# A ViT tower on one core: in the delta-rule stages, all projections ahead of the small products

## The chip, the cores and the metric

One core of a Trainium2 chip runs the whole program in one launch. The metric is the device time in microseconds (us), the median of the runs. TensorE (PE in the rows) multiplies, VectorE (DVE), ScalarE (ACT) and GpSimd (POOL) do the rest. Each works through its own list of instructions in order and waits on semaphores.

## The reference

64 images are cut into 36 patches each, embedded to 256 numbers, and get two class tokens ahead, so that there are 64 x 38 = 2432 tokens. Two layers follow. The first is causal attention and a gated mixture of eight experts, and the second, which the change touches, is a delta-rule recurrence and a ternary feed-forward block:

```python
def step(S, inp):
    qt, kt, vt, at, gkt = inp
    Sp = S * jnp.exp(gkt)[..., None]
    u = jnp.einsum('bhk,bhkv->bhv', at, Sp) + vt
    S = Sp + jnp.einsum('bhk,bhv->bhkv', kt, u)
    o = jnp.einsum('bhk,bhkv->bhv', qt, S)
    return (S, o)
...
q = silu(x @ Wq)
k = silu(x @ Wk)
v = silu(x @ Wv)
log_f = jax.nn.log_sigmoid(x @ Wf)
gamma = -jax.nn.sigmoid(x @ Wgamma)
...
a = k * gamma[..., None] * jnp.exp(gk)
out = dplr_delta_rule(q, k, v, a, gk)
```

Here k is brought to length 1 per head, gk is log_f for all 16 numbers of a head, and there are 16 heads and 38 steps.

## The kernel before

The recurrence isn't run step by step. For a pair of images and a head, the 38 steps form a triangular system, whose inverse is built row by row on VectorE (two blocks of 19 rows) and applied with small products on TensorE. The 64 images go in 8 chunks of 8 images (304 tokens). `last_layer` (line 1202) calls `delta_stage` (line 1402) eleven times, k = 0 to 10, and one stage works on four chunks at once, at different depths:

- chunk `nxt` = k: the projections of keys, queries, gamma and the forget gate. `project(n)`, n = 0 to 7, is 6 products of 128x128 by 128x304 each (line 1474), into bank 6 or 7 of the accumulators in turn. ScalarE takes the sigmoid (`sigmoid(n)`, line 1704); for n = 0 to 3 VectorE multiplies bank and sigmoid (`silu_of`, line 1856). A bank is free for the project two later when that is done: `project` 2 to 5 waits for `silu`, 6 and 7 wait for `sig`. ScalarE also copies the chunk's tokens in padded form for the next stage's values (`padded`, lines 1767 and 1769), and `key_norm` (line 1483) sums the squared keys.
- chunk `c` = k-1: `values(p)` (24 products of 128x128 by 128x272, line 1492), `sigmoid_values` (line 1694), `values_of` (line 1867), the logs of the forget gate, `decay(b)` (lines 1504 and 1506, then an exponential at line 1722), `score(p)` (line 1528) and the product of score and decay, `weigh` (line 1902).
- chunk `z` = k-2: `a_rows` (line 1549) turns the system's matrix, `inverse_row(t)` (lines 1837 and 1840) builds the inverse, and `inverse_out` with `inverse_back` (lines 1564, 1738) turn it round.
- chunk `y` = k-3: the small products. `first_half(0)` and `(1)` (line 1581) apply the first block of the inverse; ScalarE takes the result out (`first_back`, line 1746); `remainder` (line 1593) takes it to the second block; VectorE adds the values (`with_values`, line 1912); `second_half` (line 1605) applies the second block; ScalarE puts the solution in place (`solution`, line 1755) over zeros that GpSimd sets (`clear_pairs`, line 2028); `output()` (line 1621) multiplies by the queries, and `high_out` and `low_out` (lines 1777, 1922) store the sum as a high and a low part.

Stages 3 to 7 hold all four chunks. Stage 0 has only `nxt`, and stages 1 and 2 lack the small products. Stage 8 has the small products and no projections, and stages 9 and 10 hold only what is left of the last chunks. Stage 0 also computes the low-rank gate of all tokens (`low_part`, line 1539, and `low_high`, line 1730). Between stages stands a barrier of all engines.

The order within an engine is written out by hand as a list of calls: lines 1625 to 1664 for TensorE, 1781 to 1819 for ScalarE, 1950 to 1990 for VectorE, 2041 to 2063 for GpSimd. TensorE's:

```python
            first_half(0)
            first_half(1)
            project(0)
            low_part(1)
            remainder(0)
            project(1)
            low_part(2)
            remainder(1)
            project(2)
            low_part(3)
            second_half(0)
            project(3)
            low_part(4)
            second_half(1)
            project(4)
            project(5)
            output()
            project(6)
            project(7)
```

Each float32 product is shown in the trace as two weight loads and two products, so that the 64 products of `remainder(0)` are rows of x128.

Of the kernel before, what the change touches and what calls it, by code (L numbers as in the profile page):

```python
# [45 lines left out]
IP = CB // 2  # L46
# [1355 lines left out]
def delta_stage(nc, psum, bank, buffers, c, nxt, z, y):  # L1402
# [44 lines left out]
    with stage(nc, "dproj", "sig", "silu", "k_sq", "k_n2", "k_max", "k_log", "k_inv",  # L1447
# [13 lines left out]
        def _(pe):  # L1461
# [71 lines left out]
            def low_part(i):  # L1533
                if not first:
                    return
                passes = [x for k in range(HALVES) for x in split_products(
                    wgh[:, k, :], wgl[:, k, :], XH[:, k, spans[i]], XL[:, k, spans[i]])]
                for n, (left, right) in enumerate(passes):
                    mm = nc.tensor.matmul(bank[i][0:HD, 0:spans[i].stop - spans[i].start], left, right,
                                          start=(n == 0), stop=(n == len(passes) - 1))  # L1540
                mm.then_inc(g1_ready, 1)
# [84 lines left out]
            for p in range(IP):  # L1626
                values(p)
            low_part(0)
            first_half(0)
            first_half(1)  # L1630
            project(0)
            low_part(1)
            remainder(0)
            project(1)
            low_part(2)
            remainder(1)
            project(2)
            low_part(3)
            second_half(0)
            project(3)  # L1640
            low_part(4)
            second_half(1)
            project(4)
            project(5)
            output()
            project(6)
            project(7)
            key_norm(0)
            key_norm(1)
            decay(0)  # L1650
# [16 lines left out]
        def _(act):  # L1667
# [74 lines left out]
            def first_back(j):  # L1742
                if y is None:
                    return
                act.wait_ge(u1_done, j + 1)
                nc.scalar.activation(RX[:, lanes(j), :], bank[j][:, :].rearrange("p (l d) -> p l d", d=HD),
                                     ACT.Copy).then_inc(u1_back, 1)
# [36 lines left out]
                forget_parts(p)  # L1784
            forget_logs()
            nc.scalar.preload_act_table_set("sigmoid_and_others")
            first_back(0)
            sigmoid_values(0)
            sigmoid_values(1)
            first_back(1)  # L1790
            sigmoid_values(2)
            sigmoid_values(3)
            sigmoid(0)
            sigmoid(1)
            padded(0)
            sigmoid(2)
            padded(1)
            sigmoid(3)
            for i in range(len(spans)):
                low_high(i)  # L1800
            solution(0)
            solution(1)
            sigmoid(4)
            sigmoid(5)
            high_out(0)
            high_out(1)
            sigmoid(6)
            sigmoid(7)
            nc.scalar.preload_act_table_set("natural_log_exp_and_others")
            inverse_norms()  # L1810
            decay(0)
# [10 lines left out]
        def _(dve):  # L1822
# [129 lines left out]
            for t in range(1, 6):  # L1952
                inverse_row(t)
            log_forget()
            inverse_row(6)
            with_values(0)
            silu_of(0)
            inverse_row(7)
            with_values(1)
            silu_of(1)  # L1960
            values_of(0)
            values_of(1)
            inverse_row(8)
            silu_of(2)
            values_of(2)
            values_of(3)
            inverse_row(9)
            silu_of(3)
            gate_parts()
            for t in range(10, 14):  # L1970
                inverse_row(t)
            low_out(0)
# [20 lines left out]
        def _(pool):  # L1993
# [49 lines left out]
                    keys_in_pair(m, e)  # L2043
            steps(0)
            steps(1)
            clear_pairs(0)
            square(0)
            clear_pairs(1)
            square(1)
            if first:  # L2050
                pool.wait_ge(k_sq, HALVES)
                for n, part in enumerate((0, 2)):
# [190 lines left out]
```

## Time and profile before

| | |
|---|---|
| median of 3 runs | 2023.65 us (2023.57 to 2025.52) |
| the profiled execution: its own time | 2023.33 us |
| its span in the trace | 2021.3 us |
| TensorE busy | 1769.4 us (88%) |
| VectorE busy | 1084.5 us (54%) |
| ScalarE busy | 672.3 us (33%) |
| GpSimd busy | 299.6 us (15%) |
| mean granted clock of TensorE | 0.876 |
| delta stages 0 to 10 | about 1305 to 1800 us of the span |

The span is the trace of one execution; 2.0 us lie around it. A granted clock of 1.00 is 2.4 GHz and 0.50 is 1.2 GHz.

### The profile page before, as it was taken

To read this page: it belongs to the slowest core of one execution; us is meant where nothing else is said; L and a number is where in the kernel's file an instruction comes from. 1 tells how busy PE (TensorE), PEld (TensorE's weight loads), DVE (VectorE), ACT (ScalarE), POOL (GpSimd) and SP (SyncE) were. 2 spreads that over 40 slices of the span, in tenths; PEclk is the share of its full clock that TensorE was granted. 3 is DMA by queue.
4 is the path that set the end of the run, shared out by engine and by line. 5 is a ranking of instruction groups with operands and counts; after the bars stand their busy time and mean duration, and the time that the engine had idled before them with its cause. 6 is when DMAs were issued, how large, how long until landed. Compare 5 with 4: busy or idle time off the path is not lost. (4 is left out here: it accounts for less than half of the span.)

```text
span 2021.3 us, 52149 instructions
## 1 busy us (share of the span) xinstructions
PE 1769.4 (88%) x22817; PEld 1573.1 (78%) x22817; DVE 1084.5 (54%) x2346; ACT 672.3 (33%) x1389; POOL 299.6 (15%) x302
## 2 busy tenths in 40 slices
PE   5677786799999999999999999778999889777589
PEld 4466675579888999999999989566788778767468
DVE  3655555584546545545555455545534454442885
ACT  3344444432223222223223232354333333223133
POOL 0322232610000000000000000332222222100540
PEclk9788898899999999999999999788776877655579
DMA  4100000100001000000000000100000000001001
GB/s 142 50 2 1 0 0 2 65 21 22 22 1 43 1 22 21 22 22 22 22 21 22 1 1 1 34 2 2 3 4 3 3 3 4 4 4 47 1 7 44
DMA packets 9943, 36.03 MB, mean 18 GB/s; under 512 B 3056, under 2 KB 5896, under 8 KB 7176
## 3 DMA queue, kind: packets, MB, share of 16 engines
q1 hardware_dynamic: 9736, 32.96, 4.7%
q8 instruction: 167, 2.74, 0.6%
q14 instruction: 40, 0.33, 0.1%
HBM read 30.47 MB, written 2.49 MB: 16 GB/s over the span
## 5 line engine op out<-in xcount | busy, mean ns | idle before, releaser
L1042 ACT ACTIVATE hidden<-bank,moe_b 128x512 f32<-128x512 f32 (+1 forms) x320 | 213.3, 668 | 537.1 <-PE bank L934 526.1
L951 PE MATMUL bank<-moe_w2h,hidden_hi 128*128 128x256 f32 x1216 | 345.7, 284 | 0.0
L951 PE MATMUL bank<-moe_w2l,hidden_hi 128*128 128x256 f32 x1216 | 344.0, 283 | 0.0
L951 PE MATMUL bank<-moe_w2h,hidden_lo 128*128 128x256 f32 x1216 | 344.0, 283 | 0.0
L934 PE MATMUL bank<-x_hi,moe_w1h 128*128 128x512 f32 (+1 forms) x640 | 243.8, 381 | 2.9 <-ACT hidden L1042 2.8
L934 PE MATMUL bank<-x_lo,moe_w1h 128*128 128x512 f32 (+1 forms) x640 | 242.5, 379 | 0.0
L934 PE MATMUL bank<-x_hi,moe_w1l 128*128 128x512 f32 (+1 forms) x640 | 242.0, 378 | 0.0
L951 PEld LDWEIGHTS bank<-moe_w2h,hidden_hi 128*128 128x128 f32 x1216 | 233.1, 192 | 5.9 <-DVE residual L1076 4.3
L951 PEld LDWEIGHTS bank<-moe_w2l,hidden_hi 128*128 128x128 f32 x1216 | 233.2, 192 | 1.2
L951 PEld LDWEIGHTS bank<-moe_w2h,hidden_lo 128*128 128x128 f32 x1216 | 233.2, 192 | 0.0
L1076 DVE SCALAR_TENSOR_TENSOR residual<-bank,gates,residual 128x256 f32<-128x256 f32 x152 | 73.4, 484 | 290.4 <-PE bank L951 290.4
L1064 DVE TENSOR_TENSOR hidden_lo<-hidden,hidden_hi 128x512 fp32r<-128x512 f32 (+1 forms) x320 | 215.2, 672 | 11.0
L1062 DVE CAST hidden_hi<-hidden 128x512 fp32r<-128x512 f32 (+1 forms) x320 | 133.1, 416 | 87.3 <-ACT hidden L1042 79.9
L934 PEld LDWEIGHTS bank<-x_hi,moe_w1h 128*128 128x128 f32 x640 | 120.3, 188 | 25.8 <-ACT hidden L1042 5.0
L934 PEld LDWEIGHTS bank<-x_hi,moe_w1l 128*128 128x128 f32 x640 | 120.1, 188 | 20.4
L934 PEld LDWEIGHTS bank<-x_lo,moe_w1h 128*128 128x128 f32 x640 | 120.3, 188 | 18.7
L1249 POOL MEMSET gate_low<- 80x2432 f32 x1 | 2.1, 2121 | 867.1 <-POOLq L68 867.1
L167 PE MATMUL bank<-ident,normed_tiles 128*128 128x128 f32 x152 | 49.7, 446 | 47.6 <-DVE normed_tiles L136 47.6
L167 PEld LDWEIGHTS bank<-ident,normed_tiles 128*128 128x128 f32 x152 | 22.5, 204 | 74.1 <-DVE normed_tiles L136 74.0
L2008 POOL TENSOR_TENSOR decay_steps<-normed_tiles,from_here 128x304 f32<-128x304 f32 x64 | 50.5, 804 | 139.6 <-PE bank L1506 73.9
L1902 DVE TENSOR_TENSOR qk_and_ak<-bank,decay 128x304 f32<-128x304 f32 x128 | 52.2, 466 | 22.5 <-ACT decay L1722 17.0
L831 POOL TENSOR_TENSOR probs<-probs,row_inv 128x608 f32<-128x608 f32 x32 | 38.7, 1209 | 167.1 <-DVE row_inv L715 166.9
(284 smaller groups left out, 3531.5 us busy)
## 6 DMA issues: line engine op xcount, KB each, us to landing
moe_w<-in_moe_w SPq DMA_DIRECT2D x16, 1024.0 KB, 4.8
patches<-in_patches SPq DMA_DIRECT2D x8, 864.0 KB, 4.5
out<-residual SPq DMA_DIRECT2D x19, 128.0 KB, 1.7
ffn_w<-in_ffn_w SPq DMA_DIRECT2D x2, 1024.0 KB, 6.4
att_w<-in_att_w SPq DMA_DIRECT2D x1, 1536.0 KB, 5.9
delta_w<-in_delta_w SPq DMA_DIRECT2D x1, 1280.0 KB
tok_w<-in_tok_w SPq DMA_DIRECT2D x1, 768.0 KB, 4.1
delta_wvf<-in_delta_wvf SPq DMA_DIRECT2D x1, 272.0 KB
```

Source lines behind the costliest of these rows:

```text
L167: turn = nc.tensor.transpose(bank[t % 4][:, m * P:(m + 1) * P], XN[:, t % 4, m * P:(m + 1) * P], ident[:, :])
L831: nc.gpsimd.tensor_tensor(PR[:, p % 2, :, 0:SEQ], PR[:, p % 2, :, 0:SEQ], spread(RI[:, p % 2, :], 2, SEQ), ALU.mult).then_inc(normed, 1)
L934: mm = nc.tensor.matmul(bank[i % 4][:, 0:n], left, right, start=(j == 0), stop=(j == len(passes) - 1))
L951: mm = nc.tensor.matmul(bank[4 + n % 3][:, 0:D], left, right, start=(i == 0), stop=(i == len(passes) - 1))
L1042: nc.scalar.activation(H[:, i % 4, 0:n], bank[i % 4][:, 0:n], ACT.Relu, bias=b1[:, x, f:f + 1]).then_inc(acted, 1)
L1062: nc.vector.tensor_copy(HH[:, k % 2, f, 0:n], H[:, i % 4, 0:n]).then_inc(h_hi, 1)
L1064: nc.vector.tensor_tensor(HL[:, k % 2, f, 0:n], H[:, i % 4, 0:n], HH[:, k % 2, f, 0:n].bitcast(F32), ALU.subtract).then_inc(h_lo, 1)
L1076: nc.vector.scalar_tensor_tensor(out=RES[:, t, :], in0=bank[4 + n % 3][:, 0:D], scalar=G[:, t, x:x + 1], in1=RES[:, t, :], op0=ALU.mult, o ...
L1249: nc.gpsimd.memset(G1[:].bitcast(F32), 0.0).then_inc(done, 1)
L1902: nc.vector.tensor_tensor(PA[:, c % 2, p, m * HPH:(m + 1) * HPH].rearrange("p (g e) x t -> p e g x t", e=2)[:, e], psum[:, 0:PPH, n * 2 * ...
L2008: nc.gpsimd.tensor_tensor(MS[:, b % 2], spread(LZ[:, 3, b // 2, b % 2 * HPH:(b % 2 + 1) * HPH], 2, SEQ), spread(here[:, :], 1, HPH), ALU.m ...
```

## The change

No instruction is added or taken away. The four lists of calls in `delta_stage` get another order.

- TensorE: all eight projections follow the values (in stage 0 they alternate with `low_part` as before). Then come the small products without anything between them, and then norms, decays and scores as before.
- ScalarE: `sigmoid(0)` to `(3)` alternate with the sigmoids of the values, `sigmoid(4)` to `(7)` follow, and then `padded` and `first_back`.
- VectorE: `silu_of(0)` to `(3)` move ahead among the rows of the inverse, and `with_values` and `values_of` come after row 8.
- GpSimd: both squares of the keys stand ahead of both `clear_pairs`.

```diff
@@ TensorE @@
             low_part(0)
+            project(0)
+            low_part(1)
+            project(1)
+            low_part(2)
+            project(2)
+            low_part(3)
+            project(3)
+            low_part(4)
+            for n in range(4, 8):
+                project(n)
             first_half(0)
             first_half(1)
-            project(0)
-            low_part(1)
             remainder(0)
-            project(1)
-            low_part(2)
             remainder(1)
-            project(2)
-            low_part(3)
             second_half(0)
-            project(3)
-            low_part(4)
             second_half(1)
-            project(4)
-            project(5)
             output()
-            project(6)
-            project(7)
             key_norm(0)
@@ ScalarE @@
-            first_back(0)
             sigmoid_values(0)
+            sigmoid(0)
             sigmoid_values(1)
-            first_back(1)
+            sigmoid(1)
             sigmoid_values(2)
+            sigmoid(2)
             sigmoid_values(3)
-            sigmoid(0)
-            sigmoid(1)
-            padded(0)
-            sigmoid(2)
-            padded(1)
             sigmoid(3)
             for i in range(len(spans)):
                 low_high(i)
+            for n in range(4, 8):
+                sigmoid(n)
+            padded(0)
+            first_back(0)
+            first_back(1)
+            padded(1)
             solution(0)
             solution(1)
-            sigmoid(4)
-            sigmoid(5)
             high_out(0)
             high_out(1)
-            sigmoid(6)
-            sigmoid(7)
@@ VectorE @@
             log_forget()
+            silu_of(0)
             inverse_row(6)
-            with_values(0)
-            silu_of(0)
+            silu_of(1)
+            silu_of(2)
             inverse_row(7)
-            with_values(1)
-            silu_of(1)
-            values_of(0)
-            values_of(1)
-            inverse_row(8)
-            silu_of(2)
-            values_of(2)
-            values_of(3)
-            inverse_row(9)
             silu_of(3)
             gate_parts()
+            inverse_row(8)
+            with_values(0)
+            with_values(1)
+            for p in range(IP):
+                values_of(p)
+            inverse_row(9)
@@ GpSimd @@
+            square(0)
+            square(1)
             clear_pairs(0)
-            square(0)
             clear_pairs(1)
-            square(1)
```

TensorE's instructions in stage 4 (and in stages 3 and 5 to 7 alike), before, from the last value product on. One row of line 1474 is one product of a projection, and x128 of line 1581 is both first halves:

```order
L1492 MATMUL bank<-delta_wvfh,dchunk_lo 128x272
L1581 MATMUL bank<-values,inverse_t 32x16 x128
L1474 MATMUL bank<-x_hi,delta_wh 128x304
L1474 MATMUL bank<-x_lo,delta_wh 128x304
L1474 MATMUL bank<-x_hi,delta_wl 128x304
L1474 MATMUL bank<-x_hi,delta_wh 128x304
L1474 MATMUL bank<-x_lo,delta_wh 128x304
L1474 MATMUL bank<-x_hi,delta_wl 128x304
L1593 MATMUL bank<-u_then_rest,qk_and_ak 19x16 x64
```

The change, from the last products of project(7) on:

```order
L1474 MATMUL bank<-x_hi,delta_wh 128x304
L1474 MATMUL bank<-x_lo,delta_wh 128x304
L1474 MATMUL bank<-x_hi,delta_wl 128x304
L1581 MATMUL bank<-values,inverse_t 32x16 x128
L1593 MATMUL bank<-u_then_rest,qk_and_ak 19x16 x128
L1605 MATMUL bank<-u_then_rest,inverse_t 32x16 x128
L1621 MATMUL bank<-qk_and_ak 32x38 x128
L1483 MATMUL bank<-k_square_then_norm,same_head 128x304 x2
L1504 MATMUL bank<-past,ident_bf_8 128x304
L1506 MATMUL bank<-decay_steps,after 128x304
```

The 48 products of the projections stood in seven places between and behind the small ones; now 512 small products follow one another, and the key norms stand right behind the output.

ScalarE's instructions in stage 4 before, from the load of the sigmoid's table on:

```order
L1786 ACT_TABLE_LOAD
L1746 ACTIVATE u_then_rest<-bank 128x512
L1694 ACTIVATE sig_v<-bank 128x256 x2
L1746 ACTIVATE u_then_rest<-bank 128x512
L1694 ACTIVATE sig_v<-bank 128x256 x2
L1704 ACTIVATE sig_qk<-bank 128x304 x2
L1767 ACTIVATE dchunk_hi<-x_hi 128x16x19
L1769 ACTIVATE dchunk_lo<-x_lo 128x16x19
L1704 ACTIVATE sig_qk<-bank 128x304
```

The change, in the same stage (line numbers of ScalarE are 2 lower there):

```order
L1784 ACT_TABLE_LOAD
L1692 ACTIVATE sig_v<-bank 128x256
L1702 ACTIVATE sig_qk<-bank 128x304
L1692 ACTIVATE sig_v<-bank 128x256
L1702 ACTIVATE sig_qk<-bank 128x304
```

In the change one sigmoid of the values stands ahead of the first sigmoid of a projection; before, four of them and two results of `first_half` did. The copies of lines 1767 and 1769, which stood between the sigmoids, now stand behind the last one.

## Rows read from the trace of the kernel before

**Rows 1.** The page: granted clock in 40 slices of the span (50.5 us each).

```profile
PEclk9788898899999999999999999788776877655579
```

**Rows 2.** Stretches behind the values: stages 3, 4, sum of 3 to 7; stage 8.

```profile
core 0: us, PE busy (x) PEld busy (x) DVE busy (x) ACT busy (x) POOL busy (x), PEclk, DMA share, GB/s
1410.60:1447.00 36.40, 33.47 (x1074) 31.51 (x1074) 11.90 (x33) 10.78 (x30) 5.49 (x7) 0.59 0.02 4
1476.80:1510.30 33.50, 30.23 (x1073) 28.41 (x1074) 11.24 (x32) 10.78 (x30) 5.51 (x7) 0.69 0.02 4
...
sum 171.70, PE 157.62 PEld 148.37 DVE 56.76 ACT 53.94 POOL 27.47; mean PE 31.52 PEld 29.67 DVE 11.35 ACT 10.79 POOL 5.49
...
1730.00:1756.90 26.90, 19.47 (x1025) 18.49 (x1025) 8.34 (x23) 5.68 (x15) 3.26 (x4) 0.59 0.02 5
```

**Rows 3.** Timeline, PE, stage 4: start us, us, operation, xcount, [idle before <-releaser].

```profile
1503.37 1.68 PE L1621 MATMUL bank<-qk_and_ak 64*32 64x38 f32 x171
1507.43 0.95 PE L1621 MATMUL bank<-qk_and_ak 64*32 64x38 f32 x85 [2.39 <-issue]
```

**Rows 4.** By line: products of line 1474 in stages 3 to 7, duration ns min/median/max, first and last start.

```profile
L1474 PE MATMUL bank<-x_hi,delta_wl x80: 297/455/455, 1417.6 to 1700.8; 128*128 128x304 f32 x80
```

**Rows 5.** Timeline, PE, stage 8, small products without projections.

```profile
1737.51 2.31 PE L1593 MATMUL bank<-u_then_rest,qk_and_ak 32*19 32x16 f32 x128 [1.62 <-issue]
1740.98 1.48 PE L1593 MATMUL bank<-u_then_rest,qk_and_ak 32*19 32x16 f32 x79 [1.16 <-issue]
...
1744.45 3.60 PE L1605 MATMUL bank<-u_then_rest,inverse_t 32*32 32x16 f32 x128 [0.82 <-issue]
...
1755.69 1.18 PE L1621 MATMUL bank<-qk_and_ak 64*32 64x38 f32 x85 [1.86 <-issue]
```

**Rows 6.** DMA queues in the same stretch of stage 8: packets, MB, share.

```profile
q8 instruction: 8, 0.13, 2.0%
```

**Rows 7.** Timeline, stage 2, around project(2).

```profile
1367.51 1.28 ACT L1786 ACT_TABLE_LOAD   x1
...
1368.81 1.21 ACT L1694 ACTIVATE sig_v<-bank 128x256 f32<-128x256 f32 x4
1369.88 0.78 ACT L1704 ACTIVATE sig_qk<-bank 128x304 f32<-128x304 f32 x2
1370.37 0.47 DVE L1856 TENSOR_TENSOR dk_t<-bank,sig_qk 128x304 f32<-128x304 f32 x1 [2.21 <-ACT sig_qk L1704]
...
1370.90 0.41 PE L1474 MATMUL bank<-x_hi,delta_wh 128*128 128x304 f32 x1 [2.60 <-DVE dk_t L1856]
```

**Rows 8.** Busy time in stretches: stage 2 and stage 1, values' end to project(7)'s end.

```profile
1366.50:1377.80 11.30, 7.67 (x50) 6.93 (x50) 7.72 (x24) 7.28 (x20) 3.79 (x5) 1.00 0.01 1
1330.30:1341.60 11.30, 8.69 (x51) 8.44 (x50) 3.35 (x9) 7.39 (x20) 3.54 (x5) 0.85 0.00 0
```

**Rows 9.** Timeline behind the output, stage 4 (1510) and stage 8 (1756).

```profile
1510.91 0.46 DVE L1874 TENSOR_SCALAR k_square_then_norm<-bank 128x304 f32<-128x304 f32 x1
...
1513.88 0.86 DVE L1902 TENSOR_TENSOR qk_and_ak<-bank,decay 128x304 f32<-128x304 f32 x2 [0.55 <-ACT decay L1722]
...
1757.79 1.28 ACT L1809 ACT_TABLE_LOAD   x1
...
1758.92 0.56 DVE L1840 TENSOR_REDUCE inverse<-normed_tiles 128x28 f32<-128x392 f32 x1
```

**Rows 10.** Timeline, ACT: norms and padded copies, stages 0 and 2.

```profile
1322.25 0.80 ACT L1711 ACTIVATE k_square_then_norm<-k_square_then_norm 128x304 f32<-128x304 f32 x2
1322.96 0.79 ACT L1714 ACTIVATE k_square_then_norm<-k_square_then_norm 128x304 f32<-128x304 f32 x2
...
1370.48 0.51 ACT L1767 ACTIVATE dchunk_hi<-x_hi 128x304 fp32r<-128x304 f32 x1
1370.83 0.50 ACT L1769 ACTIVATE dchunk_lo<-x_lo 128x304 fp32r<-128x304 f32 x1
```

## The prediction

> **What bounds the kernel now.** I read the page first. TensorE is busy for 88% of the span, and its granted clock is 9 tenths or more in slices 9 to 25 and 6 to 8 tenths in most of the slices behind, where the delta stages lie [rows 1]. So the stages are where an order of TensorE's work can matter. I then cut each of the stages 3 to 7 behind its last value product, where the change begins, and at the end of `project(7)`. These five stretches last 36.4, 33.5, 33.6, 34.3 and 33.9 us, 171.7 together, and TensorE is busy for 157.6 of them; VectorE is for 57, ScalarE for 54 [rows 2]. TensorE's list sets the length here, not a wait for another engine. The mean clock of the first two is 0.59 and 0.69, and most projections run at the lower level, 1.2 GHz: a product's median is 455 ns, where 297 ns is the shortest [rows 4]. That is what the change can win.
>
> The timeline of TensorE shows a second thing. It stops inside runs of equal small products that wait for no other engine, with "issue" as releaser: for 2.39 us in stage 4's `output`, after 171 of its 256 products [rows 3]. Stage 8 has the same small products and no projections between them, and so shows what they do when they stand alone. There TensorE resumes from such stops at 1737.51, 1740.98 and 1744.45, that is every 3.47 us, with 128 products of 2.31 us between two stops [rows 5]. In the same 26.9 us the queue of instructions brought 8 packets with 0.13 MB, 16 KB each [rows 6], for 1025 weight loads and 1025 products [rows 2]: one packet for 128 of each. I read the stops as waits for the next packet of TensorE's own program: each block of 128 pairs takes 3.47 us or more, however fast it is multiplied. Where wide products stand between small ones, a block lasts longer than that by itself and the wait is hidden.
>
> **The change, stage 3 to 7: projections.** After the last value product, ScalarE has the logs of the forget gate and a table load, which in stage 2 ends at 1368.79, 2.2 us behind the values [rows 7]. Then one sigmoid of the values (0.3 us, from 1.21 for four), a sigmoid of 0.4 (0.78 for two) and `silu_of(0)` of 0.47 must pass, so `project(2)` starts about 3.5 us behind the values. In stage 2 it starts at 1370.90, 4.3 behind, because four sigmoids of values stand ahead [rows 7]. The other six projections take about 0.95 us each, the products at 2.4 GHz and short waits for their banks. That gives 9.2 us for all eight. Bounds: stages 1 and 2 take 11.3 from the same point, with copies and values in the way that the change moves off [rows 8]; without any wait eight would take 6.8, six starts 0.14 us apart each.
>
> **Small products.** 1024 rows of products are eight blocks. Stage 8 took 26.9 us for them, from values to the end of the output [rows 2]; TensorE was busy for 19.5 of that. A faster clock doesn't help, because the stops take what the products leave of 3.47 us: 1.16 behind `remainder` rows, 1.86 in the output [rows 5]. I take 26.9. Below it lies 24.3 (seven blocks of 3.47), above it 28.8 (eight at 3.6, the duration of a block of `second_half` at 1.2 GHz [rows 5]).
>
> So the stretch becomes 9.2 + 26.9 = 36.1 us, against a mean of 34.3 (171.7 / 5). Over five stages that is 180.5 - 171.7 = **+8.8 us**. The projections win some 3 us a stage and the small products, robbed of their cover, lose 5.
>
> The Trainium skill says on the page "TensorE: Matmul & The Clock Gate", section "Wait — 56ns, not 53.3ns?", that products never start less than about 25 ns apart. By that the 1024 small products would need about 25.6 us in either order (an estimate from the page's figure), and the change would keep all that the projections win. The trace speaks against it: 171 products of line 1621 took 1.68 us, under 10 ns each, and then a stop of 2.39 [rows 3]. A stop can be hidden by wide products; a floor for each start couldn't.
>
> **Behind the output.** Before, `project(6)`, `project(7)` and the key norms covered `high_out`, `low_out` and row 14 of the inverse, and the first `weigh` came at 1513.88, 3.6 us behind the end of the last projection at 1510.3 [rows 9]. Now nothing covers them. In stage 8 the table load ends 2.2 us behind the output and row 14 at 1759.48, 2.6 behind it [rows 9]. Then `bounded` takes 0.46, the four steps of the norms 1.5 (0.80 and 0.79 less an overlap [rows 10]) and `decay` 0.5, so the first `weigh` comes 5.0 to 5.1 behind the output: 1.5 more than now. Everything behind it stays as it is. Five stages: **+7.5 us**. Bounds 0 (the norms hide behind the decays) and 2.5 (the key norms meet the lower clock).
>
> **Other stages.** In stage 0 the four padded copies move from a covered place to between the last sigmoid and the table load, on the way to the norms. They start 0.35 us apart [rows 10]: +1.3. In stage 1 the same +1.3 stands against `project(2)` 0.7 earlier: +0.6. In stage 2 the projections also get rid of two waits for `values_of`; I put it at -0.3. Stages 8 to 10 change only in orders off TensorE's path: 0. GpSimd's squares ahead of `clear_pairs` cost nothing, since the clearing is due only at `solution`, more than 3 us behind `remainder`. `with_values` behind row 8 costs nothing either: rows 6 to 8 are done under the projections. Rows 9 to 13 and `values_of` now come behind `remainder(1)`, about 6 us of work with some 12 until the output's end; were that cover gone, the row behind it would be late by the rest.
>
> Sum: 8.8 + 7.5 + 1.6 = +17.9 us on the profiled execution's own 2023.33 us (its span is 2021.3, with 2.0 around it). That execution lies 0.3 below the median of the runs, which is nothing. **Forecast: 2041 us.**
>
> **Rivals.**
>
> *The clock decides (faster).* If the stops vanish, or don't add up, the stretch is 9.2 us of projections and small products at 2.4 GHz: about 4.5 for each of three pairs of groups, 3 for the output and 1 for the solution, 17.5 in all. With the tail's 1.5 a stage saves 34.3 - 26.7 - 1.5 = 6.1, and the kernel takes 2023 - 31 + 2 = 1994. For it speaks that projections hold the clock at 1.00 in stage 2 [rows 8]. Against it speaks that stage 8 stops just as long in rows where products are quick. It decides if blocks arrive faster than every 3.4 us. The Trainium skill's page "TensorE: Matmul & The Clock Gate", section "HAM oscillation — how this bites in real kernels", advises to keep dense products together so that the array stays at its full clock. By that rule alone this rival would win; the trace agrees with it for the projections only. Chance 0.07.
>
> *Gain and loss cancel (about the same).* Projections wait for nothing (6.8) and the tail hides the norms (0): 33.7 + 0 against 34.3, -3 us over five stages and +1.6 elsewhere, 2022. It needs ScalarE's table load to be over before `project(1)` is, and rows 7 show it 1 us too late. Chance 0.08.
>
> *The clock falls in the gap (slower still).* Between `project(1)` and `project(2)` TensorE is idle for some 1.8 us. In stage 1, with a gap of 2.6, the clock was 0.85 in the mean of the projections, in stage 2 it stayed at 1.00 [rows 8]. If it falls in each stage for the six projections behind the gap, they take 1.9 us each instead of 0.95: +5.7 a stage, 2070; if only for a part, as in stage 1, +1.7 a stage, 2050. Chance 0.13 for more than 2052.
>
> *The change doesn't do what it says.* The projections follow one another in TensorE's list, but they still wait for ScalarE and VectorE. That is in the 9.2 us.
>
> **How the numbers follow.** The forecast's case has the remaining 0.72 and a range of its own from 2031 to 2052: the projections at 8 to 11 us, the small products a microsecond to either side, the tail from 0.7 to 2.5. The range for 8 in 10 adds the milder part of the falling clock and of the cancelling case: 2026 to 2056. A measurement can tell about 0.2% from no change, 4 us. Slower by more than that: the forecast's case and the falling clock, with a part of the cancelling case off, 0.85. Within it: 0.06. Faster: 0.09.
>
> **What the changed profile would show.** In stages 3 to 7 line 1474 at a median near 300 ns; stops "issue" in lines 1581, 1593, 1605 and 1621, resumed from every 3.5 us, of 1 to 2 us each; 26 to 28 us from the first row of line 1581 to the last of 1621 in a stage; the first `weigh` 5 us behind that; 0.35 us x 4 of copies ahead of the last table load in stages 0 and 1. The prediction is wrong if the small products of a stage take under 24 us, if blocks follow closer than 3.4 us, or if the projections stay at 455 ns.

## The result, and the profile after

| | before | the change |
|---|---|---|
| median | 2024.59 us (4 runs, 2023.57 to 2027.42) | 2042.13 us (4 runs, 2039.78 to 2043.07) |
| profiled execution, own time | 2023.33 us | 2043.07 us |
| its span | 2021.3 us | 2041.1 us |

The ratio is 1.0083 with a 95% interval from 1.0065 to 1.01: slower by 17.5 us in the medians. 2041 us was forecast.

The page of the change, its row of busy times and its row of clocks:

```profile
PE 1760.4 (86%) x22817; PEld 1562.5 (77%) x22817; DVE 1087.8 (53%) x2346; ACT 672.9 (33%) x1389; POOL 299.6 (15%) x302
...
PEclk9788898999999999999999999788676867665579
```

TensorE is busy for 9 us less than before (1769.4), and the span is 19.8 us longer. So the loss is idle time. The stretches from the last value product to the end of the small products, stage 4 and the sum of stages 3 to 7 (columns as in [rows 2]):

```profile
1479.50:1514.96 35.46, 27.16 (x1073) 25.75 (x1072) 10.33 (x27) 10.35 (x27) 6.23 (x8) 0.68 0.02 4
...
sum 179.91, PE 135.11 PEld 127.63 DVE 51.62 ACT 51.73 POOL 31.14; mean PE 27.02 PEld 25.53 DVE 10.32 ACT 10.35 POOL 6.23
```

These hold the same products as the five stretches of [rows 2]. TensorE's busy time fell there from 157.62 to 135.11 us, by 22.5, and its idle time rose from 14.1 to 44.8, by 30.7. The stretches grew by the difference, 8.2 us. Both halves can be seen. First the half that was won, line 1474 in stages 3 to 7 (as [rows 4]). The last row is the longest of the waits ahead of it, 18.9 us in ten of them, with those of weight loads and products added:

```profile
L1474 PE MATMUL bank<-x_hi,delta_wh x80: 298/303/410, 1411.6 to 1692.8; 128*128 128x304 f32 x80
...
  DVE dk_t L1852: 18.9, 10
```

The median product of a projection takes 303 ns where it took 455. Then the half that was lost, TensorE's timeline in stage 4 (as [rows 3] and [rows 5]):

```profile
1482.94 0.41 PE L1474 MATMUL bank<-x_hi,delta_wh 128*128 128x304 f32 x1 [1.75 <-DVE dk_t L1852]
...
1488.67 2.70 PE L1581 MATMUL bank<-values,inverse_t 32*32 32x16 f32 x159
1492.30 2.42 PE L1581 MATMUL bank<-values,inverse_t 32*32 32x16 f32 x91 [0.94 <-issue]
...
1495.78 2.31 PE L1593 MATMUL bank<-u_then_rest,qk_and_ak 32*19 32x16 f32 x128 [0.55 <-issue]
1499.52 1.68 PE L1593 MATMUL bank<-u_then_rest,qk_and_ak 32*19 32x16 f32 x91 [1.44 <-issue]
...
1502.99 6.21 PE L1605 MATMUL bank<-u_then_rest,inverse_t 32*32 32x16 f32 x225 [0.94 <-issue]
1509.97 1.96 PE L1621 MATMUL bank<-qk_and_ak 64*32 64x38 f32 x159 [0.76 <-ACT qk_and_ak L1753]
1513.68 1.28 PE L1621 MATMUL bank<-qk_and_ak 64*32 64x38 f32 x97 [1.75 <-issue]
```

The reader is to see the points at which TensorE resumes from "issue": 1492.30, 1495.78, 1499.52 and 1502.99, that is 3.48, 3.74 and 3.47 us apart, and 1513.68, three blocks later (3.56 us each). The small products of the five stages take 27.1, 26.2, 26.9, 27.1 and 26.7 us from the end of `project(7)`.

The same trace has the packets of the queue of instructions. These are stretches of stage 4 in which a packet starts (DMA share 0.06, 14 GB/s), and the ones behind them, in which TensorE runs dry (the stretch between the two pairs, 1492.30 to 1493.40, isn't shown):

```profile
1489.90:1491.10 1.20, 1.20 (x87) 1.20 (x83) 0.00 (x0) 0.18 (x1) 0.00 (x0) 1.00 0.06 14
1491.10:1492.30 1.20, 0.27 (x17) 0.18 (x12) 0.00 (x0) 0.41 (x1) 0.00 (x0) 1.00 0.00 0
...
1493.40:1494.60 1.20, 1.20 (x56) 1.20 (x56) 0.00 (x0) 0.00 (x0) 0.00 (x0) 0.50 0.06 14
1494.60:1495.78 1.18, 0.63 (x44) 0.53 (x40) 0.00 (x0) 0.86 (x3) 0.00 (x0) 0.50 0.00 0
```

The packets start at 1489.93, 1493.44, 1496.94 and 1500.59 and take 0.9 to 1.2 us each. TensorE resumes 1.2 to 1.5 us behind the end of each, and the next packet starts 1.1 us behind that. In stages 3 to 7 all 26 stops "issue" of over 0.4 us in small products end 1.2 to 1.6 us behind the end of a packet.

And the tail of stage 4 behind the output, chosen from the timeline of all engines (as [rows 9]):

```profile
1514.89 2.40 PE L1483 MATMUL bank<-k_square_then_norm,same_head 128*128 128x304 f32 x4
1515.00 0.86 ACT L1775 ACTIVATE x_hi<-bank 128x152 fp32r<-128x152 f32 x4 [5.08 <-PE bank L1621]
...
1515.88 1.28 ACT L1805 ACT_TABLE_LOAD   x1
...
1517.49 0.85 DVE L1870 TENSOR_SCALAR k_square_then_norm<-bank 128x304 f32<-128x304 f32 x2
...
1519.42 0.85 ACT L1720 ACTIVATE decay<-bank 128x304 f32<-128x304 f32 x2
...
1519.75 1.01 PE L1528 MATMUL bank<-q_and_a,dk_in_pair 32*64 32x76 f32 x64
...
1520.85 0.85 DVE L1898 TENSOR_TENSOR qk_and_ak<-bank,decay 128x304 f32<-128x304 f32 x2 [1.32 <-PE bank L1528]
```

The output ends at 1514.96 and the first `weigh` (line 1898 now) starts at 1520.85, 5.9 us behind. It waits for the score of line 1528, which ends at 1520.75. The score comes late because the key norms and two decays ahead of it still run at the lower clock (a granted 0.50 until 1519.8): the four products of the two key norms take 2.40 us, where in the same stage of the kernel before, at the higher clock, they took 1.52, and from the first of them to the score it is 4.86 us and not 2.73.

### The profile page after: what moved, and what is told of

It is laid out like the page before. It is cut to its first block and busy times, and to the rows that moved or that the text cites. A ratio compares the mean times of both kernels' runs of the same rounds, so it can differ in the third digit from the quotient of the medians.

```text
span 2041.1 us, 52149 instructions
## 1 busy us (share of the span) xinstructions
PE 1760.4 (86%) x22817; PEld 1562.5 (77%) x22817; DVE 1087.8 (53%) x2346; ACT 672.9 (33%) x1389; POOL 299.6 (15%) x302
## 5 line engine op out<-in xcount | busy, mean ns | idle before, releaser
L167 PEld LDWEIGHTS bank<-ident,normed_tiles 128*128 128x128 f32 x152 | 22.4, 204 | 73.7 <-DVE normed_tiles L136 73.6
L1898 DVE TENSOR_TENSOR qk_and_ak<-bank,decay 128x304 f32<-128x304 f32 x128 | 52.3, 467 | 27.2 <-ACT decay L1720 17.8
L1908 DVE TENSOR_TENSOR u_then_rest<-values,bank 128x512 f32<-128x512 f32 x16 | 11.0, 689 | 103.8 <-PE bank L1593 103.8
```

Of the source, the lines that this page charges most:

```text
L167: turn = nc.tensor.transpose(bank[t % 4][:, m * P:(m + 1) * P], XN[:, t % 4, m * P:(m + 1) * P], ident[:, :])
L1898: nc.vector.tensor_tensor(PA[:, c % 2, p, m * HPH:(m + 1) * HPH].rearrange("p (g e) x t -> p e g x t", e=2)[:, e], psum[:, 0:PPH, n * 2 * ...
L1908: nc.vector.tensor_tensor(RX[:, lanes(j), :], vh_y[:, lanes(j), :], bank[j][:, :].rearrange("p (l d) -> p l d", d=HD), ALU.add).then_inc(r ...
```

## The experiments

Nine kernels ran, each beside runs of the kernel before on the same chip. Those have a median of 2026.43 us for the kernels whose names begin with e1 to e4, 2025.31 for e5 to e8 and 2023.67 for e9, and the ratios are to them. "A stage" below is the mean of stages 3 to 7 in a profile, from the last value product to the start of the next stage: 53.7 us before and 57.5 in the change.

### The change once more (`e8_change`)

> The changed kernel itself once more, on the chip of the other three, to compare them with. Both theories: 1.008 of the kernel before, 2042 us where the kernel before has 2025.

2043.89 us (2042.83 to 2048.62), ratio 1.0087 [1.007, 1.0104], a stage 57.5 us. The loss repeats.

### Is it the stops, and can they be filled? (`e2_fill`)

Twelve wide products that nobody reads are put in each of stages 3 to 7, three at each of four places: between the groups of small products, and in the middle of the output, which is cut in two for it. They are a quarter of the projections' own work.

```diff
+            def fill(n):
+                if nxt is None or y is None:
+                    return
+                pe.wait_ge(sig, 8)
+                for i in range(3):
+                    nc.tensor.matmul(bank[6][:, 0:CT], wh[:, Q, 0, 0:P], xh_c[:, 0, nxt, :],
+                                     start=True, stop=True)
...
+            fill(0)
             remainder(0)
+            fill(1)
             remainder(1)
+            fill(2)
             second_half(0)
             second_half(1)
-            output()
+            output(0)
+            fill(3)
+            output(1)
```

> The changed kernel with 12 wide products more per stage 3 to 7, whose results nobody reads: 3 each ahead of remainder(0), remainder(1) and second_half(0), and 3 in the middle of the output. Theory of supply (each block of 128 weight loads and products of TensorE's program takes 3.47 us to come, and the stops are waits for it): the extra products run inside the stops, which get shorter by as much; only the 12 pairs more of program count, 12/128 x 3.47 = 0.3 us a stage, +2 us in all. Rival (small products are slow by themselves, by a floor or by the lower clock): 12 x 0.25 = 3.0 us a stage at 1.2 GHz, +15 us in all, 2057 us.

2045.06 us, ratio 1.0093 [1.0074, 1.0113]; a stage 57.3 us, against 57.5 without the twelve. TensorE's timeline in its stage 7:

```profile
1701.80 1.13 PE L1632 MATMUL bank<-x_hi,delta_wh 128*128 128x304 f32 x3
1702.86 2.32 PE L1593 MATMUL bank<-u_then_rest,qk_and_ak 32*19 32x16 f32 x128
1705.11 1.13 PE L1632 MATMUL bank<-x_hi,delta_wh 128*128 128x304 f32 x3
1706.16 2.37 PE L1593 MATMUL bank<-u_then_rest,qk_and_ak 32*19 32x16 f32 x128
1708.47 1.13 PE L1632 MATMUL bank<-x_hi,delta_wh 128*128 128x304 f32 x3
1709.53 7.17 PE L1605 MATMUL bank<-u_then_rest,inverse_t 32*32 32x16 f32 x256
```

No stop is left in these rows. The two groups of line 1593 take 3.30 and 3.37 us with the fillers behind them, no more than a block takes alone. This is the shortest of the five stages (60.0, 56.1, 57.3, 58.2 and 55.0 us), and 11 stops of over 0.4 us remain in the five where the change has 26. Four times 1.1 us of work went into each stage, and in the mean it did not grow: in the five stretches up to the output's end TensorE is busy for 157.5 us where it was for 135.1, and they last 180.7 us where they lasted 179.9. That is the theory's +0.3 us a stage or less, and not the rival's 3.0. A time during which TensorE can do other work for nothing is a wait, and it is no cost of the small products themselves.

### Columns or instructions? (`e6_narrow`, `e7_one_pass`)

Two kernels tell what the 3.5 us belong to. The first gives each small product a quarter of its columns (4 for 16, 8 for 38 in the output). It leaves the other columns of these results out; the number of instructions is as before.

```diff
-                return slice(n, n + HD)
+                return slice(n, n + 4)
...
-                                              TS[rows, lane * HALF:lane * HALF + HB], vh_y[rows, lane, :],
+                                              TS[rows, lane * HALF:lane * HALF + HB], vh_y[rows, lane, 0:4],
```

> The changed kernel, but each small product computes a quarter of its columns: 4 of 16 in first_half, remainder and second_half, 8 of 38 in the output; the other columns are left out, so the result is not the reference's. The number of instructions is the same. Theory of supply: the stops grow by what the products lose, 26 to 27 us from the first small product to the output's end as in the change, at most 1 us less a stage, 2038 to 2042 us. Rival (the products' own columns at 1.2 GHz bound the small part): 12 to 34 ns less for each of 1024 products, 10 us or more a stage, 1990 us.

2045.25 us, ratio 1.0095 [1.0078, 1.0112]. Stage 4, TensorE:

```profile
1496.79 2.29 PE L1593 MATMUL bank<-u_then_rest,qk_and_ak 32*19 32x4 f32 x128 [0.69 <-issue]
1500.53 1.67 PE L1593 MATMUL bank<-u_then_rest,qk_and_ak 32*19 32x4 f32 x91 [1.45 <-issue]
1504.28 3.58 PE L1605 MATMUL bank<-u_then_rest,inverse_t 32*32 32x4 f32 x128 [1.23 <-issue]
...
1516.06 1.10 PE L1621 MATMUL bank<-qk_and_ak 64*32 64x8 f32 x97 [2.61 <-issue]
```

128 rows of line 1593 take 2.29 us with 4 columns and 2.31 with 16. In the output, where 38 columns became 8, the product part is shorter (1.10 against 1.28 for x97) and the stop is longer (2.61 against 1.75). TensorE resumes 3.74 and 3.75 us apart. The time is the change's too, 2045.25 against 2043.89 us, and the rival had 1990. The small products of a stage take 26.0 to 27.3 us in stages 3 to 7, as with all columns. The columns don't matter.

The second keeps the columns and halves the instructions: the operands of the small products are read to their upper 16 bits only, as bf16, so that one weight load and one product replace two of each. The result is coarser for it.

```diff
+            def top(ap):
+                return ap.bitcast(BF16)[:, 1::2]
...
-                                              TS[rows, lane * HALF:lane * HALF + HB], vh_y[rows, lane, :],
+                                              top(TS[rows, lane * HALF:lane * HALF + HB]), top(vh_y[rows, lane, :]),
```

> The changed kernel with all small products on the upper 16 bits of their operands (read as bf16), one weight load and one product instead of two of each, so half the instructions and a coarser result. Theory of supply: four blocks instead of eight, at least 13.9 us and with the waits for ScalarE and VectorE some 15 to 17 us where 26.9 were: -10 us a stage with small products, eight stages, 1960 us. Rival (the stops are something else than the supply of program): the stops stay about as they are and only the products get shorter, -3 to -5 us a stage, 2010 us.

1923.88 us, ratio 0.9487 [0.9465, 0.9508]. Stage 4, TensorE:

```profile
1476.64 1.76 PE L1584 MATMUL bank<-values,inverse_t 32*32 32x16 bf16 x128
...
1480.49 1.36 PE L1596 MATMUL bank<-u_then_rest,qk_and_ak 32*19 32x16 bf16 x97 [1.54 <-issue]
...
1483.96 1.45 PE L1608 MATMUL bank<-u_then_rest,inverse_t 32*32 32x16 bf16 x97 [1.53 <-issue]
...
1487.71 0.97 PE L1624 MATMUL bank<-qk_and_ak 64*32 64x38 bf16 x97 [1.21 <-issue]
```

The small part of a stage falls from 26.8 to between 10.7 and 12.8 us. The stops are still there and TensorE still resumes 3.47 and 3.75 us apart in this stage, every 128 products. So the time belongs to blocks of 128 weight loads and products, whatever they multiply. The 13.9 us that I had for four whole blocks were too many: the first 159 products had come in while the projections ran, so that three stops are left. The mean stage falls from 57.5 to 42.4 us, by 15 where the theory had 10, and the kernel gains 120 us and not the 82 that were expected.

### Is the tail's extra time the lost cover? (`e1_two_behind`)

`project(6)` and `project(7)` with their sigmoids go back behind the output.

```diff
-            for n in range(4, 8):
+            for n in range(4, 6):
                 project(n)
...
             output()
+            project(6)
+            project(7)
```

> The changed kernel with project(6) and project(7), and their sigmoids, back behind the output; everything else as in the change. Theory of the tail (the last two projections cover the high and low parts, row 14 and the norms): the time from the output's end to the next stage's start stays at about 21.5 us although 1.9 us of projections are now in it, and the projections ahead take 7.3 instead of 9.2 us, so about -1.7 us in each of the stages 3 to 7: -8 to -9 us against the change, 2033 us. Rival (the tail is bounded by its own work and nothing was covered): the 1.9 us only move, 2042 us.

2040.2 us (2035.42 to 2047.72), ratio 1.0085 [1.0056, 1.0115]; a stage 56.7 us. In stages 4 to 7 the time from the last projection to the next stage is 19.41, 19.41, 19.43 and 19.42 us, as it was before (19.4, in stage 5 19.0). So the two projections in front of it explain the tail. But they take 1.7 us of the stage where they stand ahead, and behind the output 3.3, 3.0, 3.3, 2.7 and 3.3 us. The timeline of stage 4 there:

```profile
1510.76 0.46 PE L1474 MATMUL bank<-x_hi,delta_wh 128*128 128x304 f32 x1
...
1512.59 0.30 PE L1474 MATMUL bank<-x_hi,delta_wl 128*128 128x304 f32 x1
1512.73 1.52 PE L1483 MATMUL bank<-k_square_then_norm,same_head 128*128 128x304 f32 x4
```

Nine of their twelve products run at 1.2 GHz in this stage, and all twelve in stages 3, 5 and 7. In the mean the tail gives back 1.95 us, the two cost 1.45 more than ahead, and the small products are 0.25 shorter. That leaves 0.8 a stage in the profile, some 4 us in all, which is too little for the ratio to show. The theory was right on the tail. Its 2033 us counted the two projections at 1.9 us, their price at the higher clock.

### The key norms ahead of the output (`e9_norms_first`)

`key_norm(0)` and `(1)` are issued ahead of `output()` in the change.

```diff
+            key_norm(0)
+            key_norm(1)
             output()
-            key_norm(0)
-            key_norm(1)
             decay(0)
```

> The change with the two key norms of the next stage issued ahead of the small products of the output, nothing else moved. In the change the first weigh of a stage comes 5.9 us behind the end of the output, and in between VectorE spends 2.4 us on the two key norms at the lower clock of the other engines' waiting time. My theory: key_norm(0) and key_norm(1) stand on VectorE's way from the output to the first weigh, so with them done beside the output the first weigh comes about 5.0 us behind the output's end, and a stage is 0.8 us shorter: 57.5 becomes 56.7 us from the end of the values to the next stage, and the kernel takes about 2038 to 2040 us where the change took 2042 to 2044. The rival: what bounds the first weigh is TensorE's own decay and score products, which begin behind the output whatever VectorE has done; then the first weigh stays at 5.9 us and the time at 2042 to 2044. In both, the small products up to the output's end keep their 26 to 27 us, and the kernel stays slower than before.

2047.66 us (2041.31 to 2048.95), ratio 1.0117 [1.0089, 1.0145], a stage 58.0 us: no gain. The step has the size that I said: in stages 4 to 7 the first `weigh` comes 4.90, 4.89, 4.89 and 4.90 us behind the output, where the change has 5.7 to 5.9. The sum isn't right. Stage 4, TensorE:

```profile
1516.84 1.09 PE L1621 MATMUL bank<-qk_and_ak 64*32 64x38 f32 x102 [1.67 <-issue]
...
1519.61 0.44 PE L1528 MATMUL bank<-q_and_a,dk_in_pair 32*64 32x76 f32 x19 [0.30 <-DVE x_lo L1918]
1520.84 0.79 PE L1528 MATMUL bank<-q_and_a,dk_in_pair 32*64 32x76 f32 x45 [0.78 <-issue]
```

A stop "issue" now falls into the 64 products of `score(0)`. The way from the first `weigh` to the next stage, which is 15.7 to 15.8 us in those stages of the change, becomes 17.4 in stages 4 and 7 and 16.9 in stage 3. In stages 5 and 6, where no stop falls there, it stays at 15.9 and the tail is 20.7. This stop, too, ends 1.5 us behind the end of a packet (1517.99 to 1519.31). So I read it that TensorE still waits for its program behind the output, and that work taken out of its way there lets it run into the next stop. The small products' part, with the norms at 2.39 us among them, is 27.2 us in the mean (26.8 in the change). Of the two theories the first was right on the 0.8 us, but wrong on the stage and on the reason. The 2.4 us of the key norms are TensorE's and not VectorE's. They stood on TensorE's own way to the decays and the score, which is what the rival named. With them gone, and the decays of stage 4 at the higher clock (0.68 us each where they took 1.22), the first `weigh` waits for ScalarE's decay. Neither theory had the stop.

### The padded copies (`e3_padded`)

The four copies of lines 1765 and 1767 return between the sigmoids.

```diff
             sigmoid(2)
             sigmoid_values(3)
+            padded(0)
             sigmoid(3)
+            padded(1)
             for i in range(len(spans)):
                 low_high(i)
             for n in range(4, 8):
                 sigmoid(n)
-            padded(0)
             first_back(0)
             first_back(1)
-            padded(1)
```

> The changed kernel with the four padded copies of ScalarE back between the sigmoids of the projections 2 and 3. Theory: stage 0 gets 1.3 to 1.7 us shorter and stage 1 some 1 us, because the copies are off the way from the last sigmoid to the norms; stages 3 to 7 do not change by more than 0.5 us each, since ScalarE has time there. In all -2 to -3 us. Rival: the copies delay project(4) and (5) as much as they delayed the norms, 0 us.

2045.2 us, ratio 1.0094 [1.0074, 1.0115]: no gain. The tail of stage 0 is 5.38 us again, where the change has 6.76, and that of stage 1 is 14.29 where it has 15.67. So the copies' 1.4 us were read rightly. But `project(5)` waits for `silu_of(3)`, whose sigmoid stands behind two of the copies, and starts 0.33 us later, and `project(6)` behind the other two starts 0.44 later. So all projections take 9.64 us where they took 9.20, in each of seven stages. Seven times 0.44 is 3.1 us; the tails of stages 0 to 2 gave back 1.4, 1.4 and 1.1. The rival holds in the sum.

### Wide products kept in the stops (`e4_split_output`, `e5_two_ahead`)

If the stops are to be filled, each group of small products must have a projection beside it. (In the kernel before the projections stood in six places between and behind the small ones, and not in seven.) One kernel starts from before and only cuts the output in four parts, with `project(4)` to `(7)` between them and behind. The other puts `project(0)` and `(1)`, whose banks are free, ahead, one projection behind `first_half`, one behind each remainder and so on, and the output in two parts with `project(6)` between and `project(7)` behind. TensorE's lists (ScalarE's and VectorE's follow the same order):

```diff
@@ from before: output in four parts @@
             project(4)
+            output(0)
             project(5)
-            output()
+            output(1)
             project(6)
+            output(2)
+            output(3)
             project(7)
@@ from the change: two ahead, the rest between @@
+            first_half(0)
+            first_half(1)
             project(2)
             low_part(3)
+            remainder(0)
             project(3)
             low_part(4)
-            for n in range(4, 8):
-                project(n)
-            first_half(0)
-            first_half(1)
-            remainder(0)
             remainder(1)
+            project(4)
             second_half(0)
             second_half(1)
-            output()
+            project(5)
+            output(0)
+            project(6)
+            output(1)
+            project(7)
```

> The kernel before, with the output cut into four parts and the projections 4 to 7 between them: second_half(1), project(4), part 0, project(5), part 1, project(6), parts 2 and 3, project(7); sigmoid(6) ahead of the high parts. Theory of supply: the stop of 1.9 to 2.4 us in each output goes, and 0.8 us for the solution stays covered: -1.5 to -2.2 us a stage, -8 to -11 us against the kernel before, 2014 us. Rival of the clock: projections between parts of the output run at 1.2 GHz where two of them ran at 2.4 GHz (+0.9 us each), which takes the gain back: 2020 to 2024 us.

2017.54 us, ratio 0.9959 [0.9945, 0.9973], a stage 53.0 us. Each theory is right in part. The stop in the output is gone in stages 4 to 7, and TensorE's idle time in the five stretches falls from 14.1 to 6.4 us. But its busy time rises from 157.6 to 161.7 us: `project(5)`, now behind a part of the output, takes 1.9 us in stage 4 and not 1.4. The profile's stages are 0.7 us shorter, less than half of what the theory had; the median gained 8.9 us on that of the kernel before, and where the rest of it lies I can't say.

> Meant to beat both kernels. project(0) and (1) stand right behind the values as in the change, where the clock is at 2.4 GHz; then both first halves; project(2), (3), (4) ahead of each remainder and of second_half, second_half(1) without a filler (a block of it lasts 3.6 us by itself), project(5), first half of the output, project(6), second half, project(7) last so that it covers the high and low parts. Theory (wide products are cheap where the clock is up, free in stops, and cover the tail): the kernel before less 1.6 us a stage for project(0) and (1) at the full clock and 1 to 2 us for the output's stop, 2010 us where the kernel before has 2024. Rival (the clock falls earlier than before, in first_half or the output, and takes it back): 2018 us, as with the split output alone.

2010.71 us (2008.36 to 2013.51), ratio 0.9926 [0.9912, 0.994], a stage 51.2 us. This is what the theory forecast. It beats both kernels, by 15 and 33 us, and computes the same. Its stretches, and TensorE in stage 4:

```profile
1472.84:1504.98 32.14, 31.05 (x1073) 29.00 (x1073) 10.63 (x30) 10.68 (x30) 5.49 (x7) 0.63 0.02 4
...
sum 158.72, PE 152.95 PEld 142.97 DVE 53.05 ACT 53.41 POOL 27.43; mean PE 30.59 PEld 28.59 DVE 10.61 ACT 10.68 POOL 5.49
```

```profile
1482.16 2.32 PE L1593 MATMUL bank<-u_then_rest,qk_and_ak 32*19 32x16 f32 x128
1484.41 0.62 PE L1474 MATMUL bank<-x_hi,delta_wh 128*128 128x304 f32 x1
...
1490.29 7.01 PE L1605 MATMUL bank<-u_then_rest,inverse_t 32*32 32x16 f32 x256
```

The mean clock of the stretch is 0.63, lower than the change's 0.68, and TensorE is busy for 152.95 us where the change needs 135.11. Yet the five stretches last 158.7 us and not 179.9, because only 5.8 are idle. Projections at 1.2 GHz that stand in the stops cost little; at 2.4 GHz and outside them each costs its full time.

## Why the prediction was right, point by point

The forecast was 2041 us and the median is 2042.13. The profiled execution's own time was put at 17.9 us more and came out 19.7 us more. That the total is so close is in part luck: two terms were 4.0 us too small together, while the stretches and the rest of the program came out 2.2 us lower. All figures in us:

| term | predicted | measured |
|---|---|---|
| eight projections, a stage | 9.2 | 9.17 to 9.24 |
| small products, a stage | 26.9 | 26.2 to 27.1, mean 26.8 |
| five stretches, sum | +8.8 | +8.2 (179.91 - 171.70) |
| behind the output, five stages | +7.5 | +10.5 |
| stages 0, 1 and 2 | +1.6 | +2.6 |
| stages 8 to 10 and the rest | 0 | -1.6, what is left of the +19.7 |

**Projections.** The gap before `project(2)` was put at 1.8 us and is 1.75. The clock is 1.00 from the last value product to the end of `project(7)` in stage 4. The rival in which it falls in the gap is false: it stayed up in all five stages, where the projections take 9.2 us.

**Small products.** That the stops add up when the wide products leave was the argument, and it held: 27 us with blocks 3.5 us apart. The reading of the stops as waits for the program's next packet rests on more than it did: filling them costs next to nothing, a quarter of the columns changes nothing, half of the instructions more than halves the time, and each stop ends 1.2 to 1.6 us behind the end of a packet. The next packet starts only 1.1 to 1.6 us behind the moment at which TensorE resumes, so that packet, wait and work follow one another round. No run brought the packets in faster or slower by themselves. That the packet is what is waited for, and not something else that comes with every 128 pairs, is therefore the best reading and not shown by a change of it alone.

**The clock decides.** False. The projections did win their clock. In the small products it didn't hold: it was 1.00 until 1492.2, then 0.52, and 0.50 from 1503 on (rows in the last section). Blocks came no faster than every 3.47 us, and this rival needed under 3.4.

**Gain and loss cancel.** False in both halves: the projections wait 1.75 us, and the tail doesn't hide the norms.

**Behind the output.** This step was mis-sized. I put the first `weigh` at 5.0 to 5.1 us behind the output by adding up ScalarE's and VectorE's steps, and it comes at 5.3 to 5.9. "The key norms meet the lower clock" stood in the text only as the upper bound, 2.5 us a stage; measured is 2.1 in the mean. The tail is 21.0, 21.7, 21.6, 21.5 and 21.6 us, where it was 19.8, 19.4, 19.0, 19.4 and 19.4. Before, the two projections ahead of the norms covered `high_out`, and in stages 4 to 7 the clock was up when they ran: in stage 4 it is 1.00 from 1503.10 to 1510.10, that is from the last product of `project(5)` on. In stage 4 of the change it is 0.50 until 4.8 us behind the output. I counted the cover alone. `e1_two_behind` has the two back and shows 19.4. `e9_norms_first` has no key norms behind the output, and where no stop falls into it its tail is 20.7. By that some 1.3 of the 2.1 us are the cover, and 0.8 the key norms and decays at the lower clock; no run takes the two apart cleanly.

**Stages 0 to 2.** The three grew by 1.7, 0.5 and 0.4 us, where +1.3, +0.6 and -0.3 were predicted. The copies cost 1.38 us in the tail of stage 0 (1.3 predicted):

```profile
1320.41 0.45 ACT L1765 ACTIVATE dchunk_hi<-x_hi 128x304 fp32r<-128x304 f32 x1
1320.76 0.45 ACT L1767 ACTIVATE dchunk_lo<-x_lo 128x304 fp32r<-128x304 f32 x1
...
1321.91 1.28 ACT L1805 ACT_TABLE_LOAD   x1
```

For stage 1 I had +0.6 and its length grew by 0.5, but not for my reasons. Behind the values it became 0.5 us shorter (projections 11.1 to 9.2, tail 14.3 to 15.7), and its values took 1.05 us longer, at a clock of 0.53 where it was 0.67. Stage 2 was wrong in its sign: from the values to the next stage it is 1.1 us longer, not 0.3 shorter (its values, at a clock of 0.61 where it was 0.52, give 0.7 of that back). The step that failed is that "the projections also get rid of two waits" is worth something there. They do (11.16 to 9.20), but VectorE sets the end of this stage. Its rows 7 and 8 now stand behind `silu_of(2)` and `silu_of(3)` and wait with them, so the first `bounded`, which all norms need, starts 15.0 us behind the values and not 13.5. This is read from the timelines; no run moved those rows alone. In stages 3 to 7 TensorE's small products hide that, as the prediction said.

**The rest.** The values of stages 3 to 7 took 0.4 us more in sum, and stage 8 took 0.7 more. What precedes stage 0 took 0.7 less, without an edit there, and what follows stage 8 took 2.0 less. That is the scatter of an execution: from the start of stage 9 to the last output this one takes 71.1 us and the kernel before 73.7, but the same kernel in `e8_change` takes 73.8.

## What to carry to other kernels

Before gathering like work on one engine, ask what its short stops cost now and who stands in them. Here TensorE was 22.5 us less busy up to the outputs' ends and the five stages were 19 us longer, since the wide products had covered the waits of the small ones. Stops that come at a fixed number of instructions, with no releaser, are room for work: put one wide group per stop, and fewer instructions are worth more than faster ones.

## What the runs showed of the hardware

**The time of 128 pairs.** Where TensorE has used up what came ahead, it resumes 3.47, 3.75 or 4.02 us apart (in the change 14, 6 and 1 times), with 128 weight loads and products between, at float32 and at bf16, and with 4, 8, 16 or 38 columns. In the small part of stage 8 of the change 7 packets of instructions came in:

```profile
q8 instruction: 7, 0.11, 1.7%
```

0.11 MB in 7 packets is 16 KB each, as in [rows 6].

**No floor of 25 ns for these products.** The Trainium skill says on the page "TensorE: Matmul & The Clock Gate", section "Wait — 56ns, not 53.3ns?", that products start at least some 25 ns apart. In the change 159 output products, of 64*32 weights each, took 1.96 us, 12 ns each, at the lower clock; the trace doesn't agree. Whether the floor holds for products on the whole array isn't shown here.

**A busy TensorE at 1.2 GHz.** The stops are the obvious suspect for the low clock in the small products. Stretches of the change in stage 4, and then one of the kernel with filled stops:

```profile
1479.50:1488.70 9.20, 7.27 (x50) 6.60 (x50) 3.23 (x11) 6.02 (x16) 2.74 (x4) 1.00 0.00 1
1488.70:1492.20 3.50, 2.67 (x160) 2.58 (x160) 0.00 (x0) 1.71 (x4) 0.00 (x0) 1.00 0.02 5
1492.30:1502.00 9.70, 7.71 (x384) 7.45 (x384) 1.34 (x2) 1.28 (x3) 1.58 (x2) 0.52 0.02 5
1502.99:1514.96 11.97, 9.46 (x482) 9.12 (x481) 4.91 (x12) 1.33 (x4) 0.92 (x2) 0.50 0.02 5
```

```profile
1702.90:1722.40 19.50, 18.24 (x779) 16.81 (x778) 7.11 (x16) 1.62 (x5) 3.50 (x4) 0.50 0.02 5
```

With the stops filled in this stage TensorE is busy for 94% of 19.5 us (18.24), and the granted clock is 0.50 all the same. The Trainium skill's page "TensorE: Matmul & The Clock Gate", section "HAM oscillation — how this bites in real kernels", puts a low clock down to gaps in which the array is idle. By that the filled kernel should run at the full clock, and it doesn't. What keeps it down between the small products wasn't tried. In stage 4 of `e1_two_behind` it came up in the tenth of the twelve wide products behind the output; in stages 3, 5 and 7 it came up only behind all twelve.
